# One step a group or two: sums and layers apart in a graph layer with routed experts

## What is computed

```python
msgs = features[edge_src] * edge_weight[:, None]
agg  = segment_sum(msgs, edge_dst)          # 12500 x 256
x    = x + agg @ W.T + b                    # features were layernorm(x)
h    = gelu(layernorm(x) @ W1 + b1)         # 256 -> 1024
probs = softmax(h @ Wg + bg); assign = argmax(probs)
x    = x + probs[assign] * (h @ Wd[assign] + bd[assign])
```

## Time and profile before

| | |
|---|---|
| median of 3 runs | 2781.99 us (2778.76 to 2784.24) |
| the profiled execution, its own time | 2780.53 us |
| its span | 2778.4 us |
| granted TensorE clock, mean over the span | 0.851 |
| busy share of the span | PE 68%, POOL 66%, DVE 39%, ACT 16% |
| first gather issued at | 76.88 us |
| last gather issued at | 2193.12 us |
| routed stage, from its first indirect gather to the end | 2302.35 to 2778.4 us |

### The profile page before, as it was taken

The page is one execution under the profiler, slowest core; times in us unless marked ns, Lnnn a source line. Parts: engine busy times, 40 slices in busy tenths (PEclk is TensorE's granted clock), DMA queues, the critical chain, the costliest instruction groups (busy, mean ns, idle before and its releaser), DMA issues.

```text
span 2778.4 us, 39308 instructions
## 1 busy us (share of the span) xinstructions
PE 1877.3 (68%) x10522; PEld 1192.6 (43%) x10523; DVE 1079.9 (39%) x3491; ACT 444.4 (16%) x847; POOL 1842.4 (66%) x1988
## 2 busy tenths in 40 slices
PE   0235675666756667666667566675667777999998
PEld 0122343333433333333334233343333446888887
DVE  8522443334433344343444234443344453333332
ACT  7000110100101001010011000110001113333332
POOL 0677777777777777777777777777777403555553
PEclk9966887888878789788888788887888888999999
DMA  9434444444444444444444344443444354555554
GB/s 396 150 103 119 149 148 120 134 148 147 149 117 132 149 149 148 119 135 147 148 149 149 104 148 149 148 149 111 141 149 149 108 204 152 182 181 179 182 179 128
DMA packets 153598, 420.31 MB, mean 151 GB/s; under 512 B 33320, under 2 KB 67499, under 8 KB 150880
## 3 DMA queue, kind: packets, MB, share of 16 engines
q0 software_dynamic: 100032, 300.27, 36.7%
q1 hardware_dynamic: 53536, 119.73, 11.7%
HBM read 328.02 MB, written 92.82 MB: 151 GB/s over the span
## 4 chain that ended last, share of the span: by engine, by line
POOL 45%; PE 27%; issue 18%; DVE 5%; DMA 2%; DVEq 1%; SPq 0%; POOLq 0%
POOL big L403 45%; PE psA L658 3%; PE psH L658 3%; PE psG L658 3%; PE psE L658 3%; PE psH L592 2%; PE psR L515 2%; PE psA L614 1%; PE psG L600 1%; PE psA L569 1%; DMA src_i<-in_srcT 1%; PE psH L648 1%; PE psE L521 1%; PE psA L648 1%; PE psE L648 1%
## 5 line engine op out<-in xcount | busy, mean ns | idle before, releaser
L403 POOL DMA_INDIRECT big<-xn_table,src_i x1664 | 1610.6, 968 | 581.5 <-issue 579.3
L515 PE MATMUL psR<-big,sel_narrow 128*32 128x256 f32 x3328 | 297.6, 519 | 597.7 <-DMA big<-xn_table,src_i 409.8
L515 PEld LDWEIGHTS psR<-big,sel_narrow 128*32 128x32 f32 x3328 | 127.1, 141 | 715.0 <-issue 630.6
L466 ACT ACTIVATE hidT<-psH,b 128x512 f32<-128x512 f32 x200 | 137.4, 687 | 1506.5 <-PE psH L592 1506.5
L592 PE MATMUL psH<-xn2T,w 128*128 128x512 f32 x800 | 374.4, 624 | 0.0
L900 DVE COPY parts<-psR 128x512 f32<-128x512 f32 x104 | 71.5, 687 | 439.0 <-PE psR L515 438.9
L521 PE MATMUL psE<-w,ident 128*128 128x512 f32 x416 | 240.8, 707 | 0.0
L592 PEld LDWEIGHTS psH<-xn2T,w 128*128 128x128 f32 x800 | 157.8, 200 | 182.6 <-issue 181.3
L894 DVE TENSOR_TENSOR place<-iota,shift_f 128x160 f32<-128x160 f32 x104 | 34.5, 332 | 328.8 <-issue 328.8
L420 POOL DMA_INDIRECT rows<-row_table,stage x105 | 104.1, 991 | 86.8 <-POOL stage L417 86.8
L417 POOL COPY stage<-rel_f 128x1 int32 (+1 forms) x105 | 19.2, 183 | 213.4 <-DVEq L1098 107.2
(11 more groups left out here) (207 smaller groups left out, 2415.2 us busy)
## 6 DMA issues: line engine op xcount, KB each, us to landing
row_table<-rows SPq DMA_DIRECT2D x25, 2064.0 KB, 8.0
big<-xn_table,src_i POOLq DMA_INDIRECT x1664
big<-in_x SPq DMA_DIRECT2D x10, 1280.0 KB, 17.4
xn_table<-big SPq DMA_DIRECT2D x10, 1280.0 KB, 13.2
big<-in_x SPq DMA_DIRECT2D x25, 512.0 KB
row_table<-big SPq DMA_DIRECT2D x25, 512.0 KB, 3.9
big<-in_Wd SPq DMA_DIRECT2D x8, 1024.0 KB, 12.7
hidT<-in_dstT SPq DMA_DIRECT2D x2, 840.0 KB, 30.5
```

The source lines that it names most:

```text
L403: nc.gpsimd.indirect_dma_start(out=xring[:, h * STEP_TILES + j, :], out_offset=None, in_=xn_dram[:, :], in_offset=bass.IndirectOffsetOnAxi ...
L466: nc.scalar.activation(hidT[:, c, :], psH[c % 2][:, :], ACT.Gelu, bias=b1[:, c:c + 1]).then_inc(s_gelu, 1)
L515: mm = nc.tensor.matmul(psQ[j * LANES:(j + 1) * LANES, o * C:(o + 1) * C], sel_narrow[:, t, :], xring[:, t, :], start=(odd == 0), stop=(od ...
```

## The change

A group now has two steps. The *sums* step of group *f* stands where the group step stood: DVE's `take_sums` and `normalize`, PE's `messages`. The *layers* step of the same group stands one gather step later, or directly before the next group's sums where those come earlier: PE's transposes, ranks, hidden columns, lists, gate and transposes of rows, with DVE's lists, `second_part` and choice. There are 152 steps; a row of the table has five integers, worked out by some ten more small DVE instructions and one more pass over 1,664 columns. The last group's two steps are written out behind the loop for its two blocks (`LAST_QB` = 2) instead of four. The two products of constants in each gather step are gone. On SP, `Wd` is loaded ahead of the two stores of the last group. Empty slots of the routed tiles now read one of 32 rows behind the last node instead of one of 128.

```diff
-COVER = 2
-STEPS = NG + NF
+STEPS = NG + 2 * (NF - 1)
...
-            store_x2(0)
-            load_x(1)
             with sp.Fori(0, NF - 2) as f:
-                store_x2(f + 1)
-                load_x(f + 2)
+                store_x2(f)
+                load_x(f + 1)
                 store_rows(f)
-            store_x2(NF - 1)
+            store_x2(NF - 2)
+            load_x(NF - 1, LAST_QB)
             store_rows(NF - 2)
...
             sp.dma_start(bd_bc, bd.rearrange("e c -> (e c)").partition_broadcast(P)).then_inc(s_bd, 16)
-            store_rows(NF - 1)
+            store_x2(NF - 1, LAST_QB)
+            store_rows(NF - 1, LAST_QB)
...
                     mm.then_inc(s_edge_mm, STEP_TILES)
 
-                    for _ in range(COVER):
-                        nc.tensor.matmul(psW[:, :], ident[:, :], w1[:, 0, 0:512], start=True, stop=True)
-
                     pe.wait_ge(s_parts, g + 1)
...
-            def transpose_xn2(f):
+            def layers(f, blocks=QB):
+                cols = blocks * P
                 pe.wait_ge(s_xn2, f + 1)
                 for k in range(KC):
-                    for q in range(QB):
+                    for q in range(blocks):
                         mm = nc.tensor.transpose(psH[k][:, q * P:(q + 1) * P],
                                                  xn2[:, q, k * P:(k + 1) * P], ident[:, :])
                     mm.then_inc(s_xt, 1)
-
-            def hidden(f, following=None):
                 rank_list(f)
+
                 pe.wait_ge(s_xtc, f * KC + KC)
                 for c in range(HC):
-                    if c == 3 and following is not None:
-                        messages(following)
                     if c >= 2:
...
                 with pe.If(kind == SECTIONS):
-                    before = n.with_bounds(min_val=0, max_val=NF - 2)
-                    hidden(before, before + 1)
-                    transpose_xn2(before + 1)
+                    messages(n.with_bounds(min_val=0, max_val=NF - 2))
                 with pe.If(kind == SECTIONS + 1):
-                    messages(0)
-                    transpose_xn2(0)
-            hidden(NF - 1)
-
-
-            rank_list(NF)
-            extend_list(NF)
+                    layers(n.with_bounds(min_val=0, max_val=NF - 2))
+            messages(NF - 1, LAST_QB)
+            layers(NF - 1, LAST_QB)
+
+            rank_list(NF, LAST_QB)
+            extend_list(NF, LAST_QB)
...
-                with dve.If(kind >= SECTIONS):
-                    g, f = step_field(load_values, k, 2, 4, DVE, NG)
+                with dve.If(kind == SECTIONS):
+                    g, = step_field(load_values, k, 2, 3, DVE, NG)
...
-                with dve.If(kind == SECTIONS):
-                    before = n.with_bounds(min_val=0, max_val=NF - 2)
-                    tie = Ticker(dve, s_rt, before * LIST_LINKS)
-                    rank_choices(tie, before)
-                    add_to_lists(tie, before)
-                    second_part(tie, before)
+                with dve.If(kind == SECTIONS + 1):
+                    f = n.with_bounds(min_val=0, max_val=NF - 2)
+                    tie = Ticker(dve, s_rt, f * LIST_LINKS)
+                    rank_choices(tie, f)
+                    add_to_lists(tie, f)
+                    second_part(tie, f)
...
+            last = NF - 1
+            link = Ticker(dve, s_ffn, last * FFN_LINKS)
+            tie = Ticker(dve, s_rt, last * LIST_LINKS)
+            take_sums(link, last, NG, last % NS * SLOT, (last - 1) % NS * SLOT + GROUP, LAST_QB)
+            normalize(link, last, LAST_QB)
+            rank_choices(tie, last)
+            add_to_lists(tie, last)
+            second_part(tie, last, LAST_QB)
+            rank_choices(tie, NF, LAST_QB)
             add_to_lists(tie, NF)
```

More of the change, by code:

```diff
@@ L202, in build @@
         span_tile, span_oct = (xn2T[:, a, 0:NG] for a in range(2))
-        u = [selv[:, a * STEPS:(a + 1) * STEPS] for a in range(7)]
+        u = [selv[:, a * STEPS:(a + 1) * STEPS] for a in range(9)]
         small = xn2T[:, :, :].rearrange("p a b -> p (a b)")
@@ L541, in gather_step, with rank_list @@
                     pe.sem_inc(s_placed, 1)
-            def rank_list(b):
+            def rank_list(b, blocks=QB):
                 pe.wait_ge(s_chosen, b + 1)
@@ L599, in hidden @@
                     cg = c % 4
-                    mm = nc.tensor.matmul(psG[cg * GATE_COLS:(cg + 1) * GATE_COLS, :], wg[:, c, :], hidT[:, c, :],
-                                          start=(c < 4), stop=(c >= 4))
+                    mm = nc.tensor.matmul(psG[cg * GATE_COLS:(cg + 1) * GATE_COLS, 0:cols], wg[:, c, :],
+                                          hidT[:, c, 0:cols], start=(c < 4), stop=(c >= 4))
                 mm.then_inc(s_gp, 1)
[L603 to L610, removed]
+                for i in range(2 * blocks):
+                    half, q = i // blocks, i % blocks
                     if i >= 2:
@@ L935, in take_sums, with rank_choices @@
                                              None, ALU.add))
[L937 removed]
+            def rank_choices(tie, b, blocks=QB):
                 dve.wait_ge(s_chosen, b + 1)
@@ L995, in choose, with normalize @@
+                nc.vector.tensor_tensor(chosen[:, 0:blocks, :], route_b[:, 0:blocks, :],
+                                        valid[:, bass.ds(f * QB, blocks)].unsqueeze(2).to_broadcast([P, blocks, E]),
                                         ALU.mult).then_inc(s_chosen, 1)
-            def normalize(link, f):
+            def normalize(link, f, blocks=QB):
                 dve.wait_ge(s_z, f + 1)
                 dve.wait_ge(s_xg, f * 16 + 16)
-                x2 = xg[:, :, :]
-                for a in range(2):
+                x2 = xg[:, 0:blocks, :]
+                for a in range(blocks // 2):
@@ L1016, in normalize, with second_part @@
                 o.then_inc(s_xn2, 1)
-            def second_part(tie, f):
+            def second_part(tie, f, blocks=QB):
                 dve.wait_ge(s_rows_free, f + 1)
                 dve.sem_inc(s_pass_dve, 1)
-                for i in range(2 * QB):
-                    half, q = i // QB, i % QB
+                for i in range(2 * blocks):
+                    half, q = i // blocks, i % blocks
                     dve.wait_ge(s_tr, f * (2 * QB) + i + 1)
```

196 lines of the change are left out of this document (97 added, 99 removed).

## The result

The changed kernel takes 2819.2 us (median of 4 runs, 2816.0 to 2821.2) against 2783.1 for the kernel before (4 runs); the ratio is 1.0122 (95% interval 1.0109 to 1.0135). It is slower, as forecast, but by 36 us where 15 were forecast. The profiled execution took 2821.2 us, 25 more than the sum of its terms (2795.9).

A forecast was written before the change was run, and what follows sets the result against it. POOL's gathers bound the loop before, PE's and DVE's chain after: loop 36.4 us and following chain 13 longer, tail 34 shorter, list +15.4, so 2797 us; range 2761 to 2845, forecast's own 2788 to 2820.

The forecast's parts named there:

- What bounds: In the loop, POOL's gathers (20.36 us a step) set the pace before; after, PE's and DVE's chain, POOL waiting some tens.
- The interval: One group's chain in the loop, four gather steps: 85.6 us against 81.4 of gathers; 23 intervals, engines 36.4 us later.
- I cost its going at nothing, and bound it by the 1.7 us: Removing the filler (products of constants) from each gather step costs nothing, within 1.7 us either way.
- the term of 7.1: Closing gather step, its products to the end of DVE's one-hots: 3.64 products, 0.76 copy, 0.1 to spreading, 2.63 after: 7.1 us.
- The ranks' 2.59: PE's ranks in the layers step, behind the transposes: 2.59 us.
- the forecast's sum for PE and DVE alone: Engines' time between group 0's and group 23's sums: 23 x 85.6 + 5 x 8.5 = 2011.3 us, against 1974.9 of gathers.
- The rule of the Trainium skill: Short bursts of PE products with waits between fall back to the low clock; it speaks against the change, sum stays.
- The first rival: Loop: gathers stay the bound, with closing-step products at the high clock, interval 82.2 us; 2761 us, 28 in 100.
- The second rival: Layers step: low clock reaches further into hidden columns, restart longer, interval 2 us longer; 2843 us, 13 in 100.
- The tail: From step 101's products: 75.7 us (62.6 before) to the last one-hots, then 48.6 (82.8 before) to the sorted list.
- SP's order: Wd's loads ahead of the last two stores: hidden, last store done 6 us before the list; uncovered, at most some 10.
- The sensitivity: One microsecond an interval is 23 us at the end, as long as the engines set the pace; even at 84.9.

The follow-up runs named there:

- experiments 2 and 3: 2: kernel before without the two products of constants, 2783.9 us; 3: half the gathers left out, changed kernel 2769.6 us, kernel before 2417.4 us.
- experiment 1: Changed kernel with the two products of constants (filler) back behind the products of each gather step, ahead of the spreading: 2792.5 us.
- Experiment 4: Changed kernel with three products of constants ahead of PE's wait for the copy of the sums, in each sums step: 2791.1 us, ratio 1.0025.
- experiment 6: Changed kernel with two products of constants behind the spreading of each gather step: 2762.1 us, ratio 0.9926.

## Where the prediction was right, and where it went wrong

- *What bounds.* Right: POOL before, PE's and DVE's chain after (experiments 2 and 3).
- *The interval.* The mechanism was right, a term mis-sized: 85.6 forecast, 86.5 measured, and 23 intervals multiply the 0.9 us to 21 of the 25 us. By the terms, as means over the groups: products to one-hots 7.9 instead of 7.1; transposes and ranks 5.0 instead of 4.6; hidden columns to the choice 27.4 instead of 27.1; the sums 22.5 instead of 23.0; the rest as forecast within 0.2. The last gather is issued at 2236.4 us, where the text named 2219.
- *The step that failed* is "I cost its going at nothing, and bound it by the 1.7 us", with the term of 7.1 that goes with it. The 7.1 mixed two clocks: products at the low level, but 2.63 behind them from a row in which the filler had just run, so that the spreading took 1.01; without it, 1.74 in the mean. It took what the filler's going saves (0.1 between the end of the copy, 749.63, and the spreading, where the earlier trace rows had it at 751.29) and not what it costs. The ranks' 2.59 came from a row partly at the high level too; here they take 3.3. The products of the closing step were put at the low level with or without filler; with it they take 2.0 in the mean of the intervals with four steps (experiment 1), which I had not looked for. In the chain as it now is, its going costs 27 us (experiment 1), three quarters of the whole loss.
- *What the filler does not explain alone.* With half the gathers and no filler, the loop takes 2011.4 us, where the forecast's sum for PE and DVE alone was 2011.3. So close a match is in part luck: against the forecast, the terms from the choice to the place columns (4.7 for 5.3) and of the sums (22.6 for 23.0) are shorter, those of ranks, transposes and hidden columns longer. But it shows that the forecast let the gathers and the chain run beside each other at no cost to either, and that the chain is 19.3 us longer with all gathers. How much of these 19.3 us is the same loss as the filler's is open; the spreading of the closing step is shorter in both runs.
- *The rule of the Trainium skill* ("TensorE: Matmul & The Clock Gate", section "HAM oscillation") was weighed the right way round, and then not followed to its end: I applied it to the products and not to the spreading and ranks. Experiment 4 agrees with it: the same products took 6.06 us in the mean behind an idle wait and 3.66 behind filler.
- *The first rival* (the gathers stay the bound, 2761 us) did not hold in the changed kernel, whose closing products take 3.6 us. With filler behind the spreading they fall to 2.0, transposes, ranks and hidden columns fall too, and the time is 2762.1 (experiment 6): its price was right.
- *The second rival* (the low clock reaches further, 2843 us) did not come in its size: its sign was over 29 us from the first hidden column to the choice, and it is 27.4. What it had right is the direction, in the spreading and the ranks.
- *The tail.* Right within 3.3 us of 124: 78.3 for 75.7, 49.3 for 48.6. *SP's order*: hidden, as forecast.
- *The sensitivity.* 23 us for each us of the interval stood in the text, and yet the forecast's own range allowed the interval 0.4 us less and 1.0 more. The time lies inside the forecast's own range (2788 to 2820), at its upper end.

Not settled: how much filler is needed, where exactly it is best, and how the gathers lengthen the chain. Which part of the split's 16 us an interval belongs to the lost interleaving and which to the clock is known only in sum: with half the gathers, 6.9 us return with filler behind the spreading.

## What to carry to other kernels

Where an edit moves a chain from under another engine's cover, each row taken from the old trace has to be checked for what ran just before it there: the same 32 products took 1.93 or 3.64 us in this kernel. A product of constants that nothing reads was worth tens of microseconds here where the chain was the bound and nothing where the gathers were, so it is to be judged again whenever the bound changes. And an interval that repeats 23 times turns a 1% error of its length (0.9 of 85.6 us) into more than the 15 us of the whole forecast effect.

## What was not expected of the hardware

The place of the filler counted: the same two products gave 27 us back ahead of the spreading and 57 us behind it, where the gathers bind again. Transposes (1.97 to 1.45 us in the mean, 1.04 at best) and ranks, those of 8 columns from 1.85 to 1.07 in the mean, get shorter as well with the filler right before them.
